# Layer 0's expert network: shared expert first, first matmuls of seven halves ahead of the router's shares

## What is computed

```python
x = x + jnp.tanh(g_ffn[0]) * _L0_ffn_ref(_layernorm(x), ...)   # layer 0, second half

def _L0_ffn_ref(x, ...):              # DIM 128, INTER 64, N_EXPERTS 16, TOPK 4
    scores = sigmoid(xt @ gate_w.T)
    _, idx = top_k(scores + gate_b, 4)
    w = take_along_axis(scores, idx); w = w / sum(w) * 2.5
    comb = zeros((T, 16)).at[arange(T)[:, None], idx].add(w)
    for e in range(16):               # every expert sees every token
        gate, up = split(xt @ w13[e].T, 2)
        y = y + comb[:, e, None] * ((silu(gate) * up) @ w2[e].T)
    gate, up = split(xt @ w13_s.T, 2) # the shared expert, with no share
    return y + (silu(gate) * up) @ w2_s.T
```

## Time and profile before

| | us |
|---|---|
| median of 3 executions | 669.22 |
| lowest, highest | 668.12, 670.95 |
| span of the profiled execution, first to last instruction | 666.6 |
| PE busy in that span | 527.9 (79%) |
| DVE busy | 386.9 (58%) |
| ACT busy | 328.5 (49%) |
| mean granted clock of PE | 0.893 |

### The profile page before, as it was taken

The page is one execution under the profiler, slowest core; times in us unless marked ns, Lnnn a source line. Parts: engine busy times, 40 slices in busy tenths (PEclk is TensorE's granted clock), DMA queues, the critical chain, the costliest instruction groups (busy, mean ns, idle before and its releaser), DMA issues.

```text
span 666.6 us, 15622 instructions
## 1 busy us (share of the span) xinstructions
PE 527.9 (79%) x5272; PEld 403.1 (60%) x5272; DVE 386.9 (58%) x1148; ACT 328.5 (49%) x953; POOL 219.3 (33%) x409
## 2 busy tenths in 40 slices
PE   2968878876879996999999998999997720799930
PEld 1623245544744535788888887888886420799930
DVE  1699845557365543777877877787786350122212
ACT  2646734344121223887787877778785210222210
POOL 8384722124100000534344443444433016000025
PEclk9798977899868997999999999999999575699985
DMA  9985543333199925000004999000001971200012
GB/s 275 232 236 144 156 155 110 98 113 92 33 233 225 207 72 224 2 2 3 1 0 107 228 230 179 2 2 1 0 0 32 425 304 51 68 17 17 17 36 67
DMA packets 46839, 73.32 MB, mean 110 GB/s; under 512 B 4613, under 2 KB 40374, under 8 KB 45638
## 3 DMA queue, kind: packets, MB, share of 16 engines
q1 hardware_dynamic: 42588, 59.93, 35.9%
q0 software_dynamic: 1472, 8.72, 3.6%
q10 hardware_dynamic: 2730, 4.03, 2.0%
HBM read 69.06 MB, written 3.60 MB: 109 GB/s over the span
## 4 chain that ended last, share of the span: by engine, by line
PE 49%; DVE 20%; ACT 11%; DMA 6%; issue 6%; POOL 6%; POOLq 1%; ACTq 0%; SPq 0%; DVEq 0%
PE ps L1541 9%; ACT work L833 6%; PE ps L1555 5%; PE ps L1677 4%; PE ps L1478 4%; PE ps L1667 4%; DMA work<-in_kv_blk 3%; PE ps L1512 2%; PE ps L1586 2%; POOL xe_scratch L720 2%; DVE ps L1164 2%; DVE sumsq L958 2%; POOL early_w L725 2%; PE ps L1415 2%; PE ps L1358 2%
## 5 line engine op out<-in xcount | busy, mean ns | idle before, releaser
L833 ACT ACTIVATE work<-ps,nb,rkey 125x56 f32<-125x56 f32 x576 | 176.3, 403 | 52.1 <-DVE nb L1167 44.9
L1541 PE MATMUL ps<-work,region 128*64 128x96 f32 (+1 forms) x2304 | 116.7, 252 | 7.0 <-DVE work L1227 4.8
L1541 PEld LDWEIGHTS ps<-work,region 128*64 128x64 f32 (+1 forms) x2304 | 99.5, 137 | 18.7 <-issue 5.2
L1555 PE MATMUL ps<-region,work 125*64 125x129 f32 x1152 | 72.5, 273 | 4.6 <-POOL work L686 3.1
L686 POOL TENSOR_TENSOR work<-work,rs 125x336 f32<-125x336 f32 x96 | 71.9, 749 | 7.5
L1555 PEld LDWEIGHTS ps<-region,work 125*64 125x64 f32 x1152 | 64.1, 136 | 5.4 <-POOL work L686 3.6
L684 POOL TENSOR_TENSOR rs<-rs,rkey 125x6 f32<-125x6 f32 x96 | 19.2, 201 | 123.8 <-DVE rs L1179 123.8
L1164 DVE TENSOR_REDUCE ps<-ps 125x6 f32<-125x336 f32 x96 | 48.9, 510 | 17.9 <-PE ps L1541 17.4
L1175 DVE TENSOR_REDUCE sm<-work 125x6 f32<-125x336 f32 x96 | 47.4, 494 | 1.2 <-ACT work L833 0.6
L725 POOL DMA_INDIRECT early_w<-ys_scratch,gidx x14 | 13.4, 958 | 83.3 <-DMA ys_scratch<-folded 79.4
L1386 PE MATMUL ps<-xln,folded 128*128 128x448 f32 x64 | 29.9, 592 | 9.5 <-ACT region L760 9.5
(11 more groups left out here) (296 smaller groups left out, 1037.9 us busy)
## 6 DMA issues: line engine op xcount, KB each, us to landing
region<-in_w SPq DMA_DIRECT2D x6, 2048.0 KB, 19.5
region<-in_ctxT SPq DMA_DIRECT2D x16, 750.0 KB
early_w<-in_ctx SPq DMA_DIRECT2D x16, 672.0 KB
region<-in_ctx SPq DMA_DIRECT2D x16, 672.0 KB
work<-in_ctxT_blk SPq DMA_DIRECT2D x22, 187.5 KB
early_w<-in_w POOLq DMA_DIRECT2D x1, 4096.0 KB, 12.4
region<-in_ctx_blk ACTq DMA_DIRECT2D x11, 187.5 KB
early_w<-in_ctx_blk ACTq DMA_DIRECT2D x10, 187.5 KB
```

The lines of the kernel that those rows point to most:

```text
L833: i = act.activation(shares_of(a, h)[:, c, :], ps[:CP, 2 + 2 * a + h, c * S:(c + 1) * S], ACT.Exp, bias=nb[:, a, q:q + 1], scale=rkey[:, b ...
L1541: mm = pe.matmul(ps[r0:r1, 2 + 2 * a + h, c * S:c * S + WIDE], keysT[:, s, c0 + r0:c0 + r1], qT[:, p, a * S:a * S + WIDE], start=True, sto ...
L1555: mm = pe.matmul(ps[i * COL:(i + 1) * COL, bank, 0:KW], A[:CP, i, h, c * S:c * S + COL], keys[:, 2 * p + i, h * CH + c, :], start=(h == 0 ...
```

## The change

The 18 steps get a new order: the shared expert is now j = 0 and 1, and the pairs are j = 2 to 17. `hh` has six buffers. On PE, `hidden(0)` to `hidden(6)` and the shared expert's two `down` stand ahead of the transposes, `hidden(7)` right behind them; from then on PE is six `hidden` ahead of `down` in place of one. On DVE the product of silu and up (now `ffn0_up(j)`, L1115) is parted from the multiplication by the shares (`ffn0_share(j)`, L1121). Five `ffn0_up` stand inside the router's chain and two right behind it, ahead of the copies to `combT`. The reciprocal `rkey` moves from between chain and copies to the loop, behind j = 9. No operation is added or taken away.

```diff
+FFN0 = 2 * (PAIRS + 1)
+HH_BUFS = 6
+FIRST_UP = 7
-        hh = [carve(HALF, "early") for _ in range(2)]
+        hh = [carve(HALF, "early") for _ in range(HH_BUFS)]
...
+            def ffn0_up(j):
+                p = F0 if j < 2 else 128
+                v.wait_ge(e0_act, j + 1)
+                if j >= HH_BUFS:
+                    v.wait_ge(e0_y, j - HH_BUFS + 1)
+                v.tensor_tensor(hh[j % HH_BUFS][:p, :], sg[j % 2][:p, :], ps[:p, 2 * (j % 2) + 1, 0:HALF], ALU.mult).then_inc(e0_up, 1)
+            def ffn0_share(j):
+                v.wait_ge(e0_up, j + 1)
+                v.wait_ge(e0_share, j - 1)
+                v.tensor_tensor(hh[j % HH_BUFS], hh[j % HH_BUFS], ps[:, 6 + j % 2, 0:HALF], ALU.mult).then_inc(e0_h, 1)
...
             for k in range(1, TOP0):
                 step(v.tensor_tensor(hot[:, :, :], over_tiles(iota_e[:, 0:E0]), bcast(idxf[:, :, k], E0), ALU.is_equal))
                 step(v.tensor_tensor(msk[:, :, :], msk[:, :, :], hot[:, :, :], ALU.add))
+                ffn0_up(k - 1)
...
             step(v.tensor_scalar(den[:, :], den[:, :], ROUTE, None, ALU.mult))
+            ffn0_up(3)
...
                 if r + 32 < PARTS:
                     step(v.tensor_tensor(msk[:, :, :], msk[:, :, :], parts[:, :, r:r + E0], ALU.subtract))
+                if r == 32:
+                    ffn0_up(4)
             v.sem_inc(comb_ok, 1)
-            v.wait_ge(rk_sd, 1)
-            v.reciprocal(rkey[:, :, :], rms[:, :, :]).then_inc(rk_ok, 1)
+            for j in range(5, FIRST_UP):
+                ffn0_up(j)
             v.wait_ge(combT_mm, 1)
             for h in range(2):
                 v.tensor_copy(combT[:PARTS, half(h)], ps[:PARTS, 6 + h, 0:HALF]).then_inc(combT_ok, 1)
...
+            for j in range(2, FFN0):
+                ffn0_share(j)
+                if j + FIRST_UP - 2 < FFN0:
+                    ffn0_up(j + FIRST_UP - 2)
+                if j == 9:
+                    v.wait_ge(rk_sd, 1)
+                    v.reciprocal(rkey[:, :, :], rms[:, :, :]).then_inc(rk_ok, 1)
...
             hidden(0)
             hidden(1)
+            pe.wait_ge(ld_ffn0, 32)
+            pe.wait_ge(sc0_ok, 1)
+            for j in range(2):
+                hidden(j + 2)
+                down(j)
+            for j in range(4, FIRST_UP):
+                hidden(j)
             pe.wait_ge(comb_ok, 1)
...
+            hidden(FIRST_UP)
             pe.wait_ge(combT_ok, 2)
-            shares(0)
+            shares(2)
...
-            for j in range(last):
-                if j + 1 < last:
-                    if j:
-                        hidden(j + 1)
+            for j in range(2, FFN0):
+                if j + 1 < FFN0:
                     shares(j + 1)
+                if j + FIRST_UP - 1 < FFN0:
+                    hidden(j + FIRST_UP - 1)
                 down(j)
```

More of the change, by code:

```diff
@@ L811, in _ @@
             act.activation(sc0[:, :, :].rearrange("p n e -> p (n e)"), ps[:, 4, 0:NT * E0], ACT.Sigmoid).then_inc(sc0_ok, 1)
-            for j in range(2 * (PAIRS + 1)):
-                p = 128 if j // 2 < PAIRS else F0
+            for j in range(FFN0):
+                p = F0 if j < 2 else 128
                 act.wait_ge(e0_mm, j + 1)
@@ L1133, in _ @@
                 v.tensor_copy(combT[:PARTS, half(h)], ps[:PARTS, 6 + h, 0:HALF]).then_inc(combT_ok, 1)
[L1135 to L1145, removed]
+            for j in range(2, FFN0):
[5 more added lines that the diff above has]
+                    v.reciprocal(rkey[:, :, :], rms[:, :, :]).then_inc(rk_ok, 1)
+            v.wait_ge(e0_y, FFN0)
             for h in range(2):
@@ L1470, in hidden @@
             def hidden(j):
-                pair, h = divmod(j, 2)
-                p = 128 if pair < PAIRS else F0
+                h = j % 2
+                p = F0 if j < 2 else 128
                 if j >= 2:
@@ L1476, in hidden @@
                 for g in range(2):
-                    w = w13[:, g, pair * 2 * F0:(pair + 1) * 2 * F0] if pair < PAIRS else ws[:, g * F0:(g + 1) * F0]
+                    w = ws[:, g * F0:(g + 1) * F0] if j < 2 else w13[:, g, (j // 2 - 1) * 2 * F0:j // 2 * 2 * F0]
                     mm = pe.matmul(ps[:p, 2 * (j % 2) + g, 0:HALF], w, xln[:, half(h)], start=True, stop=True)
@@ L1481, in shares, with down @@
             def shares(j):
[L1483 to L1490, removed]
+                if j >= 4:
+                    pe.wait_ge(e0_h, j - 3)
+                pe.matmul(ps[:, 6 + j % 2, 0:HALF], pair_sel[:PARTS, j // 2 - 1, :], combT[:PARTS, half(j % 2)],
+                          start=True, stop=True).then_inc(e0_share, 1)
+            def down(j):
+                if j < 2:
+                    pe.wait_ge(e0_up, j + 1)
+                else:
+                    pe.wait_ge(e0_h, j - 1)
+                w, x = (w2s[:, :], hh[j][:F0, :]) if j < 2 else (w2p[:, j // 2 - 1, :], hh[j % HH_BUFS])
+                pe.matmul(ps[:, 4 + j % 2, 0:HALF], w, x, start=(j < 2), stop=(j >= FFN0 - 2),
+                          skip_group_check=True).then_inc(e0_y, 1)
             hidden(0)
             hidden(1)
+            pe.wait_ge(ld_ffn0, 32)
[5 more added lines that the diff above has]
+                hidden(j)
             pe.wait_ge(comb_ok, 1)
@@ L1501, in _ @@
             mm.then_inc(combT_mm, 1)
+            hidden(FIRST_UP)
             pe.wait_ge(combT_ok, 2)
-            shares(0)
[L1505 to L1515, removed]
-            for j in range(last):
-                if j + 1 < last:
-                    if j:
-                        hidden(j + 1)
+            shares(2)
+            for j in range(2, FFN0):
+                if j + 1 < FFN0:
                     shares(j + 1)
+                if j + FIRST_UP - 1 < FFN0:
+                    hidden(j + FIRST_UP - 1)
                 down(j)
-            pe.wait_ge(e0_h, 2 * PAIRS)
+            pe.wait_ge(e0_h, FFN0 - 2)
             pe.matmul(ps[:, 6, 0:128], wq1[:, :], wk1[:, :], start=True, stop=True).then_inc(g1_mm, 1)
```

## The result

The changed kernel takes **663.4 us** (median of 14 executions, 658.53 to 667.77) against 668.67 for the kernel before (14 executions, 664.03 to 674.78). The ratio is 0.9918 with a 95% interval of 0.9892 to 0.9944, which is 3.7 to 7.2 us less. Forecast were 7.2 us less for the stage, and 662.0 us for the time.

A forecast was written before the change was run, and what follows sets the result against it. The stage was bound by DVE's router chain, then PE alone at 2.45 us per step, then a tail. Stage end 208.6 + 30.2 + 0.35 = 239.15 against 246.35, 7.2 us less; span 659.4 plus 2.6 gives 662.0; range 659.0 to 665.7.

The forecast's parts named there:

- PE beside the router: From 190.71, seven hidden and two down run without a gap until 206.35; clock full from 196.24 on.
- the prices behind a change of shape: Beside the router, hidden and down taken at 1.65 and 0.95 us, instead of 1.50 and 0.76.
- The router with five products: DVE's router chain with five ffn0_up inside: last part at 204.9, shares ready 6.3 us later than before.
- PE's slack: Shares are ready before PE gets there at 206.35; 1.4 us of slack cover their delay.
- To the first shares: Transposes from 206.35, hidden(7) to 208.5, copies to combT end at 208.55; PE loses some 0.2 us.
- The loop: 16 shares, ten hidden, 16 down: 30.2 us without waits, plus some 0.35 for the last product's way through DVE.
- The ledger: PE before, 55.6 us: 45.0 full-clock work; 2.8 first half-clock stretch, 4.6 router gaps, 2.3 later half clock, 1.3 idle.
- What lies around the span: Time outside the profiled span: 2.6 us, taken from the median, added to a span of 659.4.
- The rivals: Held by the router, 667.4, chance 0.08; slower, 672.4, 0.04; more than forecast, 660.3, 0.05.
- slower: PE, ACT and DVE form a ring; clock doesn't rise beside the router; 672.4 us, chance 0.04.
- more: Clock rises 2 us earlier and shapes cost nothing: 1.0 + 0.7, giving 660.3 us; chance 0.05.
- signs of being wrong: PE idle ahead of transposes or first shares, 0.50 slices after 200, loop steps above 2.45 us, later give-back.

The follow-up runs named there:

- the swaps: Changed kernel with copies to combT ahead of the seventh silu-up product, and shares of j = 13 ahead of the product for j = 17: stage 48.81 us.
- The spare products in the kernel before: Kernel before plus three spare matmuls, results unread, in the layer norm ahead of the router: stage 55.15 us, against 55.44 and 55.03.
- spare products: Changed kernel plus three spare matmuls, results unread, in the layer norm ahead of the router: stage 48.02 us; timed 659.35 us, ratio 0.9872 to the kernel before.

## Why the prediction came out as it did

The time lies in the range (659.0 to 665.7), and the direction and the mechanism were forecast. The size of the gain was not met as well as the time: 7.2 us against 5.3 between the medians. That the time is only 1.4 off is in part luck, since the kernel before was counted from 669.22 (3 executions) and has 668.67 in 14. By its steps:

- **PE beside the router: right.** `hidden(4)` to `(6)` were to end 15.44 us behind the sigmoid's start; PE turned to the transposes at 207.67, which is 15.50. Small misses cancel in this: the prices behind a change of shape, 1.65 and 0.95, were 1.70 and 0.95, and the last three halves took 4.67 for 4.50, but the clock rose 4.8 us behind the sigmoid and not 5.3, worth 0.25. It did not fall again in the stage. The recorded sum also has the two shared halves end at 196.65 where its own terms give 196.77.
- **The router with five products: right.** `ffn0_up(1)` was to wait 1.35 us and waited 1.28; the shares were to be ready 14.0 us behind the sigmoid and were at 14.0 (205.92 + 0.26 - 192.17); PE's slack was to be 1.4 and was 1.5. The Trainium skill, "TensorE: Matmul & The Clock Gate", section "Architectural detail: the array is 16× 32×32, not 1× 128×128", has DVE as strict first-in first-out; the trace agrees, the comparison at L1133 starting only behind the waiting product.
- **To the first shares: too short by 0.3 us.** I had the silu follow PE at once; it started at 207.87, 0.2 behind the point at which PE turned to the transposes, and the copies with it.
- **The loop: mis-sized by 0.6 us.** 30.55 was forecast and it took 31.16 (210.19 to 241.35). I had counted that a product waits for the `down` that frees its buffer, here `ffn0_up(17)` for `down(11)`, but not that the shares for j = 13 stand behind it on DVE while PE already needs them: a wait on one engine held the next piece of work, which is the very thing I had looked for in the router and not in the loop. With the swaps the same stretch takes 30.76 (205.15 to 235.91), so this wait is 0.4 of the 0.6; the other 0.2 stay with the swaps, where two of the last `down` take 0.85 and 0.87 instead of 0.76. Ahead of the first shares the swaps save another 0.35 (1.99 us from PE's turn to the transposes, against 2.34).
- **The ledger: wrong in two lines.** It put 2.8 us of the kernel before down to the first stretch at half clock. The spare products in the kernel before show that it cost nothing, and that the whole of that time belongs to the router's gaps. And it has 1.3 us of idle time ahead of the last `down`, where PE was in fact busy with the other `down` for most of that time and idle for 0.39 us (rows below). The sum rested on neither, since the time after was built up forward. Its check by the ledger carries the 2.8 over into the kernel after, where PE is on the path; there spare products gave back 1.2.
- **What lies around the span:** 1.7 to 1.9 us in the runs (665.8 against a span of 664.1, 658.87 against 657.0), not the 2.6 taken.

The end of the stage in the timeline of the kernel before, for the second of the ledger's lines:

```profile
243.93 1.02 PE L1512 MATMUL ps<-early_w,w2s 64*128 64x448 f32 x2
...
245.33 1.02 PE L1512 MATMUL ps<-early_w,w2s 64*128 64x448 f32 x2 [0.39 <-DVE early_w L1140]
```

So of the 7.2 us, 6.0 are in the stage on the mean of two profiles of each kernel. The 1.2 lacking are the 0.3 and the 0.6 above, 0.2 by which the mean of the kernel before lies under the 55.44 that I counted from, and 0.1 by which the second profile of the kernel after lies above the first on the mean. The timed gain, 5.3 us between the medians, agrees with 6.0 within its interval of 3.7 to 7.2; the forecast 7.2 is at the edge of that interval. The span was to be 659.4 and is 664.1 in this profile: 0.9 of that is the stage, the rest the 3.8 us around it. A border of the clock ahead of the stage and one behind it took 1.3 and 1.6 of these; only the later ones had been left in the range, with 1.5 us of either sign.

The rivals fell: the clock rose and stayed, the router's slack held, nothing came out slower, and the time isn't near the 660.3 of "more". Two of the prediction's signs of being wrong did show, both small: PE idle for 0.37 us ahead of the first shares, and in this pair of profiles 2.5 us given back by later stages, of which 1.6 go with the time at which the clock fell.

## What to carry to other kernels

When an engine waits for a chain on another engine, work for it is found only if that other engine also frees its buffers from within the chain; count each such insertion as a wait at the head of a queue, in the chain and in the last steps of the loop behind it. In this kernel a stretch at half clock cost nothing where TensorE waited anyway (55.15 us against 55.03 and 55.44) and 1.2 us where TensorE was on the path: check which engine ends last there before paying for it or counting it as a gain. Once TensorE is on the path, idle places in which the clock would fall can be worth filling, even with products that nobody reads, as long as these are not themselves in the way, as they were ahead of the first scores.

## What the runs showed of the hardware that I had not expected

- Spare matmuls whose results nobody reads held the granted clock at 1.00 through a layer norm and the router in every slice from 176 to 244; without them, in the first profiles of both kernels, it was at 0.50 from 186.0 to 196.2 and from 183.3 to 197.0. The Trainium skill, "TensorE: Matmul & The Clock Gate", section "What's actually happening", says that activity releases the throttle; the trace agrees, as the same kernel had 0.50 there without the added matmuls and 1.00 with them.
- With the clock at 1.00 throughout, the stage was the same to the hundredth in the two profiles of that kernel, 48.02 us. Where the clock fell and rose in or ahead of it, two profiles each gave 55.03 and 55.44, and 49.18 and 49.35.
- The time ahead of the stage does not repeat: among the nine profiles without spare products the sigmoid started between 185.6 and 193.5 us, and the part from the first scores on took 401.3 to 410.2 us, with no instruction changed in either. A change of a few microseconds in one stage is therefore read better from that stage than from the whole time.
